# Self-attention P.V with two products instead of three, and a new order of work at the end and the start of each batch

## The chip, the cores and the metric

The kernel runs on one core of one Trainium2 chip. The metric is the device time of one execution in microseconds (us). TensorE (PE) multiplies, VectorE (DVE) and ScalarE (ACT) read its results out of the eight PSUM banks, GpSimd (POOL) works on SBUF alone, and SyncE (SP) issues the DMAs. Each engine runs its own list of instructions in order; semaphores tie the lists together.

## The reference, cut to what matters

The layer takes x (8 batches of 128 tokens, 512 features) and a context of the same size and computes

```
x = x + self_attention(layernorm(x))      # 32 query heads of 16, 8 key/value heads, rotary angles, causal
x = x + cross_attention(layernorm(x), ctx) # 32 query heads of 128, 4 key/value heads
x = x + ffn(layernorm(x))                  # two branches, one scaled by a routing weight, layer norm with gamma, beta
```

All data are float32. In the self-attention of one batch (the code splits its 32 heads into 8 groups j of 4 query heads that share one key/value head):

```
scores[h] = q[h] @ k[h // 4].T / 4, masked above the diagonal
attn[h]   = softmax(scores[h])
ctx[h]    = attn[h] @ v[h // 4]            # the product P.V
out       = concat(ctx) @ Wo.T
```

For the cross-attention, "latents" are the normalised rows of x after the self-attention; keys and values are made from the context rows followed by the latents, so every batch's latents must be turned (transposed) and multiplied by the key and value weights.

## The kernel before, in words

**Number format.** Every float32 operand a of a product is split into two fp32r parts: the high part h, which ScalarE's copy rounds, and the low part l = a - h, which VectorE makes from the same PSUM bank. `split3` (L235 to L239) then issues three matmuls: high by high (L237), high by low, low by high. So each PSUM result that is used again costs one ScalarE copy (L1285) and one VectorE subtraction (L1597).

**Phases.** The kernel has a start (weights and context are turned), the self-attention in 8 batches (`batch(b, last)` in each engine's list, about 98 to 290 us), the cross-attention in 128 steps, and the ffn. The change touches only the start and the 8 batches.

**One batch on TensorE (L890 to L988).** Eight steps j. Step j turns the normalised probabilities of group j (`turn(j)`, L903, four 128x128 transposes into bank 5 or 6), then does other work of the batch, then `values(j-1)`: the product P.V of the group before, into bank 7. The values lie block-diagonally in `Vbdh` and `Vbdl`, so that the 128 output rows are filled by the eight groups one after the other, and each group costs a `split3` of 512 columns (for j = 7, two of 256 columns, each as soon as its half of the low part `PTal` is there). The other work:

- step 0: `unit(U_B0 + 2 * b)` (12 matmuls: cross-attention values of the batch's context rows, XTh and XVh in the rows), then `turn_xn(b + 1)` (L789: the next batch's normalised x into bank 0), then `scores(b, 2)`;
- steps 2 to 4: `q_product`, `scores(b, 3)` and `kv_product` (next batch's queries, keys, values);
- steps 6 and 7: `turn_q` and `turn_k` (L810, L817) of the next batch, into banks 1 and 4;
- after step 7: `values(7)`, `scores(b + 1, 0)`, the output product (12 matmuls with `SOh`, into bank 6), `scores(b + 1, 1)`, the tail unit `unit(U_B0 + 2 * b + 1)` (12 matmuls, XTh and XKh in the rows), and `turn_latents(b)` (L829: the rows xn2 into bank 0).

`scores(b, m)` (L856 to L874) starts two banks with the mask (L864, two matmuls) and adds three products of 64 rows each for both halves (L868, L871, L874, two matmuls each); it uses the banks 2, 3 and 4 in turn.

**The followers.** ScalarE's list for a batch (L1352 to L1379): for each j the high part `PTah` of the turned probabilities, then the exponentials `probs(b, j + 3)` (four activations, each with an accumulator read, L1342); in step 0 also the high parts of the unit and of `turn_xn`; after step 7 the high part of the keys, of the attention output (OTh) and of the values, `probs(b + 1, 0..2)`, the high part of the tail unit and of the latents. VectorE's list (L1729 to L1796): for each j the row maxima (L1721), the low part `PTal`, the reciprocals of the sums (L1727); the rotary products; after step 7 the low parts of the keys, their block-diagonal copies `Kbdl` (L1696, four per batch), the low part of the output OTl, `maxima(b + 1, 0)` and `(b + 1, 1)`, the low part of the values. Then VectorE waits for the output product, adds it to x (L1785), takes the statistics (L1629 to L1633), and only then `reciprocals_a(b + 1, 1)` and `maxima(b + 1, 2)` (L1789), the normalised rows xn2 (L1791), two more `Kbdl`, and the low parts of the tail unit and of the latents. GpSimd multiplies the probabilities by the reciprocals (L635), makes the high block-diagonal keys `Kbdh` (L620) and the inverse standard deviations (L600, L651).

**The last batch** has no next batch: its steps 1, 2 and 4 to 7 hold units of the earlier latents instead (`LAST_STEPS`, L451), and after the tail unit come `first_queries(0)` and `turn_latents(7)`.

Of the kernel before, what the change touches and what calls it, by code (L numbers as in the profile page):

```python
# [29 lines left out]
ALU = mybir.AluOpType  # L30
# [34 lines left out]
def decoder_layer(nc, x, ctx, s_wq, s_wk, s_wv, s_wo, x_wq, x_wk, x_wv, x_wo, gate_w, up_w, down_w,  # L65
                  fc1_w, fc2_w, expert_w, gamma, beta, rope, out):
    with ExitStack() as stack:
# [74 lines left out]
        VBW = P + SD  # L142
        Vbdh = sb("Vbdh", "F", 0, [SKV * VBW], F32R)
        Vbdl = sb("Vbdl", "F", 4.5, [SKV * VBW], F32R)
        OTh, OTl = PTah[:, 0, :], PTal[:, 0, :]
# [108 lines left out]
        v_ptl_half, v_ol_half = sem("v_ptl_half"), sem("v_ol_half")  # L254
# [211 lines left out]
        def _(sp):  # L466
# [52 lines left out]
            sp.wait_ge(pe_pv, NB)  # L519
# [66 lines left out]
        def _(gp):  # L586
# [51 lines left out]
            def batch(b, last):  # L638
                for j in range(2, SKV):
                    normalise(b, j)  # L640
                    if j == 3 and b + 2 < NB:
                        inv_std1(b + 2)
# [128 lines left out]
        def _(pe):  # L771
# [84 lines left out]
            def scores(b, m):  # L856
# [6 lines left out]
                for bk, _ in halves:  # L863
# [8 lines left out]
                pe.wait_ge(v_kbd, KC * b + m + 1)  # L872
# [17 lines left out]
            def batch(b, last):  # L890
# [16 lines left out]
                def values(j):  # L907

                    if j == SKV - 1:
                        for n, split in enumerate((v_ptl_half, v_ptl)):  # L910
                            pe.wait_ge(split, SKV * b + SKV if n else b + 1)
                            cols = slice(n * KEYS, (n + 1) * KEYS)
                            op = split3(pe, bank[7][:, cols], Vbdh[:, j * P:(j + 1) * P], Vbdl[:, j * P:(j + 1) * P],
                                        PTah[:, j % 2, cols], PTal[:, j % 2, cols], False, n == 1)
# [3 lines left out]
                    if j == 0:  # L918
# [3 lines left out]
                    op = split3(pe, bank[7][:], Vbdh[:, j * P:(j + 1) * P], Vbdl[:, j * P:(j + 1) * P],  # L922
                                PTah[:, j % 2, :], PTal[:, j % 2, :], j == 0, False)

                for j in range(SKV):
                    turn(j)
                    if j == 0:
# [41 lines left out]
                else:  # L969
                    unit(U_L0 + 6)  # L970

                for g in range(SG):
                    if g % 2 == 0:
                        pe.wait_ge(v_ol if g else v_ol_half, b + 1)
# [1096 lines left out]
```

## Time and profile before

| | us |
|---|---|
| median of 3 runs (lowest, highest) | 1007.47 (1006.96, 1007.87) |
| time of the profiled execution | 1007.5 |
| its span, first to last instruction | 1005.8 |
| mean granted TensorE clock | 0.999 |

The span is what the trace shows; 1.7 us of the profiled execution's own time lie around it. The profile page gives each engine's busy time. A busy TensorE is not TensorE at its peak, since matmuls overlap and their ends are modelled: the distance from one start to the next says what a matmul costs. "mean ns of one" is therefore longer than the cost of a matmul in a row of many.

### The profile page before, as it was taken

What the parts mean: (1) busy time and instruction counts of PE and PEld (TensorE: products, weight loads), DVE (VectorE), ACT (ScalarE), POOL (GpSimd) and SP (SyncE); (2) the same over time, 40 slices, a digit from 0 to 9 for tenths busy, and PEclk for the clock granted to TensorE, in tenths of its full rate; (3) what the DMA queues carried; (4) which work ended last, traced back from release to release, by engine and by line L of the source; (5) the groups of instructions that cost most, each with busy time, mean ns of one, the idle gap of its engine ahead of it and who ended that gap; (6) DMA issues with size and microseconds to landing.
All of it is one profiled execution on the core that took longest, in us unless ns stands there. A gap on an engine that the chain in (4) does not pass through costs nothing.

```text
span 1005.8 us, 16102 instructions
## 1 busy us (share of the span) xinstructions
PE 995.6 (99%) x5552; PEld 836.7 (83%) x5552; DVE 641.4 (64%) x1224; ACT 559.5 (56%) x1695; POOL 519.8 (52%) x529
## 2 busy tenths in 40 slices
PE   8999999999999999999999999999999999999997
PEld 7777777777788888888888888888888888899996
DVE  6888888888433786555655655555555566655654
ACT  5766667666534665555656556555655667422221
POOL 3645444444231786665755756576666568512220
PEclk9999999999999999999999999999999999999999
DMA  9410111104454313233213313322332245100000
GB/s 343 119 29 15 43 42 44 42 22 124 135 157 119 95 57 102 74 95 105 86 61 105 105 64 106 92 76 94 95 105 75 83 139 168 62 22 21 21 22 21
DMA packets 74857, 85.15 MB, mean 85 GB/s; under 512 B 4512, under 2 KB 54688, under 8 KB 74784
## 3 DMA queue, kind: packets, MB, share of 16 engines
q1 hardware_dynamic: 74784, 84.21, 26.2%
q8 instruction: 42, 0.69, 0.3%
q14 instruction: 31, 0.25, 0.1%
HBM read 65.32 MB, written 18.87 MB: 84 GB/s over the span
## 4 chain that ended last, share of the span: by engine, by line
PE 92%; DVE 3%; ACT 2%; DMA 1%; issue 1%; POOL 1%; SPq 1%; DVEq 0%; POOLq 0%; ACTq 0%
PE bank L237 23%; PE bank L239 22%; PE bank L238 22%; PE bank L1143 11%; PE bank L1187 5%; PE bank L903 3%; PE bank L864 1%; PE bank L868 1%; DMA rawO<-in_L_attn_Wo_dram 1%; PE bank L871 1%; PE bank L874 1%; ACT Pb L1424 0%; DVE Kbdl L1696 0%; PE bank L817 0%; PE bank L810 0%
## 5 line engine op out<-in xcount | busy, mean ns | idle before, releaser
L673 POOL TENSOR_TENSOR Pb<-Pb,b_rec 128x512 f32<-128x512 f32 x128 | 135.5, 1059 | 200.6 <-DVE b_rec L1848 200.5
L1424 ACT ACTIVATE Pb<-bank,b_nb 128x256 f32<-128x256 f32 x256 | 119.1, 477 | 14.3 <-DVE b_nb L1843 14.2
L1843 DVE TENSOR_REDUCE b_nb<-bank 128x2 f32<-128x512 f32 x128 | 88.1, 688 | 59.2 <-PE bank L239 58.4
L635 POOL TENSOR_TENSOR Pa<-Pa,a_rec 128x512 f32<-128x512 f32 x64 | 68.2, 1066 | 102.1 <-DVE a_rec L1727 101.5
L1342 ACT ACTIVATE Pa<-bank,a_nb 128x128 f32<-128x128 f32 x256 | 90.8, 370 | 45.5 <-DVE a_nb L1721 44.8
L1285 ACT ACTIVATE PTh<-bank 128x512 fp32r<-128x512 f32 x128 | 76.3, 596 | 67.1 <-PE bank L1187 67.1
L237 PE MATMUL bank<-WOh,Oh 128*128 128x512 f32 x256 | 111.3, 435 | 0.0
L1597 DVE TENSOR_TENSOR PTl<-bank,PTh 128x512 fp32r<-128x512 f32 x128 | 87.7, 686 | 22.3 <-ACT PTh L1285 22.2
L239 PE MATMUL bank<-WOh,Ol 128*128 128x512 f32 x256 | 101.0, 395 | 0.0
L238 PE MATMUL bank<-WOl,Oh 128*128 128x512 f32 x256 | 100.4, 392 | 0.0
L1285 ACT ACTIVATE Oh<-bank 128x512 fp32r<-128x512 f32 x64 | 38.3, 599 | 91.4 <-PE bank L239 91.4
L1597 DVE TENSOR_TENSOR Ol<-bank,Oh 128x512 fp32r<-128x512 f32 x64 | 44.2, 690 | 63.1 <-ACT Oh L1285 63.1
L1187 PE MATMUL bank<-ident,Pb 128*128 128x128 f32 x512 | 76.8, 272 | 0.0
L239 PE MATMUL bank<-KV,Ql 128*128 128x256 f32 x256 | 72.4, 283 | 0.0
L238 PE MATMUL bank<-KV,Qh 128*128 128x256 f32 x256 | 72.3, 282 | 0.0
L237 PE MATMUL bank<-KV,Qh 128*128 128x256 f32 x256 | 71.8, 281 | 0.0
L1187 PEld LDWEIGHTS bank<-ident,Pb 128*128 128x128 f32 x512 | 61.4, 140 | 8.8 <-POOL Pb L673 0.2
L1285 ACT ACTIVATE PTah<-bank 128x512 fp32r<-128x512 f32 x72 | 43.4, 603 | 32.2 <-PE bank L903 24.1
L679 POOL TENSOR_TENSOR rstd<-var_eps,half 128x1 f32<-128x1 f32 x16 | 12.3, 767 | 92.4 <-DVE var_eps L1633 92.4
L1597 DVE TENSOR_TENSOR PTal<-bank,PTah 128x512 fp32r<-128x512 f32 (+1 forms) x88 | 50.3, 587 | 11.3 <-ACT PTah L1285 10.6
L239 PEld LDWEIGHTS bank<-WOh,Ol 128*128 128x128 f32 x256 | 48.0, 188 | 11.3
L1424 ACT ACTIVATION_READ_ACCUMULATOR Pb<-bank,b_nb 128x1 f32 x256 | 53.6, 210 | 0.0
(279 smaller groups left out, 3008.6 us busy)
## 6 DMA issues: line engine op xcount, KB each, us to landing
KV<-kv_scratch SPq DMA_DIRECT2D x64, 512.0 KB, 3.4
kv_scratch<-KVst SPq DMA_DIRECT2D x64, 256.0 KB, 3.1
raw<-in_L_xattn_Wo_dram SPq DMA_DIRECT2D x32, 256.0 KB, 3.9
raw<-in_L_xattn_Wq_dram SPq DMA_DIRECT2D x24, 256.0 KB, 3.2
cx<-in_ctx_dram SPq DMA_DIRECT2D x8, 256.0 KB, 8.9
raw_first<-in_L_xattn_Wq_dram SPq DMA_DIRECT2D x8, 256.0 KB, 4.6
raw<-in_L_ffn_up_w_dram SPq DMA_DIRECT2D x8, 256.0 KB, 3.9
raw<-in_L_ffn_down_w_dram SPq DMA_DIRECT2D x8, 256.0 KB, 3.5
```

What stands on the lines that cost most here:

```text
L237: pe.matmul(dst, lh, rh, start=start, stop=False)
L238: pe.matmul(dst, lh, rl, start=False, stop=False)
L239: return pe.matmul(dst, ll, rh, start=False, stop=stop)
L635: gp.tensor_tensor(pj, pj, a_rec[:, SG * j:SG * j + SG].unsqueeze(2).to_broadcast([P, SG, P]), ALU.mult).then_inc(g_norm, 1)
L673: gp.tensor_tensor(pk, pk, b_rec[:, k % 4, :].unsqueeze(2).to_broadcast([P, 2, KEYS]), ALU.mult).then_inc(b_g_norm, 1)
L1143: op = pe.matmul(bank[6][:], lhs[:, p, kc, :], rhs[:, kc, :], start=p in (0, 4, 5) and kc == 0 and n_op == 0, stop=kc == 1 and n_op == 2, ...
L1187: op = pe.transpose(bank[3 + k % 2][:, c * KEYS + h * P:c * KEYS + (h + 1) * P], Pb[:, k % 4, h, c * P:(c + 1) * P], ident[:])
L1285: return act.activation(dst, src, ACT.Copy)
L1342: op = act.activation(Pa[:, j % PS, c * P:(c + 1) * P], bank[2 + j % 3][:, c * P:(c + 1) * P], ACT.Exp, bias=a_nb[:, h:h + 1], scale=1.0, ...
L1424: op = act.activation(Pb[:, k % 4, h, :], bank[k % 3][:, h * KEYS:(h + 1) * KEYS], ACT.Exp, bias=b_nb[:, k % 4, h:h + 1], scale=1.0, accum ...
L1597: return dve.tensor_tensor(dst, src, f32(hi_part), ALU.subtract)
L1843: dve.tensor_reduce(b_nb[:, k % 4, :], bank[k % 3][:].rearrange("p (h k) -> p h k", h=2), AX.X, ALU.max, negate=True).then_inc(b_v_nb, 1)
```

## The change

**Two products instead of three.** One tile `Vst` holds, for each group j, the high values in the 16 columns of row block j and the low values 64 columns further (for j < 4) or 64 columns nearer (for j >= 4). One product of `Vst` with `PTah` and one with `PTal` then give the high part's result in one half of the bank's partitions and the low part's result in the other half. Groups 0 to 3 go to bank 7 and groups 4 to 7 to bank 4. The low half must be moved by 64 partitions and added: ScalarE copies it out (`OLa`, `OLb`), and `add_low(n)` multiplies it with a shifted identity `swap_r` of 64 rows and adds it into the other half of the same bank. The high and low parts of the output are then made for the two halves separately.

**Order.** The tail unit goes ahead of the output product. `turn_latents(b)` leaves the end of batch b for step 0 of batch b + 1; it stands behind the unit and waits until the low part of the turned x (`v_xnl`) has left bank 0. `turn_xn` goes ahead of the unit. Keys are turned into bank 3. SP's load of the gate and expert weights waits for the last output product.

**GpSimd** makes the fourth low diagonal block (m = 3), behind `normalise(b, 2)`.

```diff
         # turn_k, scores
+                if b:
+                    pe.wait_ge(a_exp, SKV * b)
-                    op = pe.transpose(bank[4][:, m * P:(m + 1) * P], kr[:, m * P:(m + 1) * P], ident[:])
+                    op = pe.transpose(bank[3][:, m * P:(m + 1) * P], kr[:, m * P:(m + 1) * P], ident[:])
...
+                    if m == 0 and n:
+                        pe.wait_ge(v_qkl, 2 * b + 2)
+                    if m == 1 and n == 0 and b:
+                        pe.wait_ge(v_ol, 2 * b)
...
         # values, TensorE
+                    bk = bank[7] if j < 4 else bank[4]
...
-                    op = split3(pe, bank[7][:], Vbdh[:, j * P:(j + 1) * P], Vbdl[:, j * P:(j + 1) * P],
-                                PTah[:, j % 2, :], PTal[:, j % 2, :], j == 0, False)
+                    if j == 4:
+                        pe.wait_ge(a_exp, SKV * b + 6)
+                    pe.matmul(bk[:], Vst[:, j, :], PTah[:, j % 2, :], start=j % 4 == 0, stop=False)
+                    op = pe.matmul(bk[:], Vst[:, j, :], PTal[:, j % 2, :], start=False, stop=j == 3)
+                    if j == 3:
+                        op.then_inc(pe_pv, 1)
+
+                def add_low(n):
+                    pe.wait_ge(a_ol, 2 * b + n + 1)
+                    bk, rows, low = ((bank[7], UPPER, OLa), (bank[4], LOWER, OLb))[n]
+                    pe.matmul(bk[:], swap_r[rows, :], low, start=False, stop=True,
+                              skip_group_check=True).then_inc(pe_sw, 1)
...
         # step 0, TensorE
-                        unit(U_B0 + 2 * b)
+                        pe.wait_ge(v_vl, b + 1)
                         if not last:
-                            if b:
-                                pe.wait_ge(v_htl, b)
-                            else:
+                            if b == 0:
                                 pe.wait_ge(v_ctl, 6)
                             turn_xn(b + 1)
+                        unit(U_B0 + 2 * b)
+                        if b:
+                            if not last:
+                                pe.wait_ge(v_xnl, b + 2)
+                            turn_latents(b - 1)
                         scores(b, 2)
...
+                    if j == 6:
+                        add_low(0)
...
         # after step 7, TensorE
+                add_low(1)
+                tail = U_E0 - 1 if last else U_B0 + 2 * b + 1
+                pe.wait_ge(v_ol, 2 * b + 1)
+                if b:
+                    pe.wait_ge(v_htl, b)
+                unit(tail)
+                pe.wait_ge(v_ol, 2 * b + 2)
                 for g in range(SG):
...
                 if not last:
                     scores(b + 1, 1)
-                unit(U_E0 - 1 if last else U_B0 + 2 * b + 1)
-                if not last:
-                    pe.wait_ge(v_vl, b + 2)
-                else:
+                if last:
                     first_queries(0)
                     pe.wait_ge(v_ul, U_L0 + 7)
-                turn_latents(b)
+                    turn_latents(b)
...
         # ScalarE, batch
+                    if j == 0 and not last:
+                        xn_hi(b + 1)
+                    if j == 5:
+                        act.wait_ge(pe_pv, 2 * b + 1)
+                        hi(OLa, bank[7][UPPER, :]).then_inc(a_ol, 1)
+                    if j == 7:
+                        if not last:
+                            k_hi(b + 1)
+                        act.wait_ge(pe_sw, 2 * b + 1)
+                        hi(OTh[LOWER, :], bank[7][LOWER, :]).then_inc(a_o, 1)
                     if j + 3 < SKV:
                         probs(b, j + 3)
                     if j == 0:
                         unit_hi(U_B0 + 2 * b)
-                        if not last:
-                            xn_hi(b + 1)
+                        if b:
+                            latents_hi(b - 1)
...
-                act.wait_ge(pe_pv, b + 1)
-                hi(OTh, bank[7][:]).then_inc(a_o, 1)
+                act.wait_ge(pe_pv, 2 * b + 2)
+                hi(OLb, bank[4][LOWER, :]).then_inc(a_ol, 1)
                 if not last:
                     values_hi(b + 1)
+                act.wait_ge(pe_sw, 2 * b + 2)
+                hi(OTh[UPPER, :], bank[4][UPPER, :]).then_inc(a_o, 1)
...
         # VectorE, batch
+                    if j == 0 and not last:
+                        ln1_lo(b + 1)
                     if j < 4:
                         reciprocals_a(b, j + 2)
                     if j == 0:
                         unit_lo(U_B0 + 2 * b)
+                        if b:
+                            latents_lo(b - 1)
...
-                    diagonal_keys(b + 1, (2, 3))
+                    diagonal_keys(b + 1, (2,))
                 unit_lo(U_E0 - 1 if last else U_B0 + 2 * b + 1)
-                latents_lo(b)
+                if last:
+                    latents_lo(b)
```

VectorE's wait for the output product, the addition, the statistics and `maxima(b + 1, 2)` behind them stay in their order.

## Rows read from the trace of the kernel before

**Rows 1.** The page's first part: each engine's busy time, share and instructions.
```profile
PE 995.6 (99%) x5552; PEld 836.7 (83%) x5552; DVE 641.4 (64%) x1224; ACT 559.5 (56%) x1695; POOL 519.8 (52%) x529
```

**Rows 2.** Busy time by stretch, one batch; then clock, DMA share and GB/s.
```profile
157.90:187.80 29.90, 29.89 (x170) 23.05 (x169) 25.81 (x56) 20.18 (x80) 14.08 (x14) 1.00 0.13 36
```

**Rows 3.** TensorE's groups by shape, whole span: count | busy us, mean ns.
```profile
L239 PE MATMUL bank<-PTah,Vbdl 128*128 128x512 f32 x56 | 22.0, 393 | 0.0
L239 PE MATMUL bank<-PTah,Vbdl 128*128 128x256 f32 x16 | 4.5, 282 | 0.0
```

**Rows 4.** Timeline, TensorE, end of a batch and start of the next: start, duration.
```profile
180.14 0.40 PE L874 MATMUL bank<-Kbdl,QTh 64*128 64x512 f32 x2
180.47 0.50 PE L237 MATMUL bank<-SOh,PTah 128*128 128x512 f32 x1
...
183.10 0.39 PE L239 MATMUL bank<-SOh,PTal 128*128 128x512 f32 x1
183.32 0.61 PE L864 MATMUL bank<-mask_r,ident_r 128*128 128x512 f32 x2
...
184.76 0.50 PE L237 MATMUL bank<-XTh,XKh 128*128 128x512 f32 x1
...
187.62 0.60 PE L829 MATMUL bank<-ident,xn 128*128 128x128 f32 x4
...
188.05 0.60 PE L903 MATMUL bank<-ident,Pa 128*128 128x128 f32 x4
188.41 0.47 PE L237 MATMUL bank<-XVh,XTh 128*128 128x512 f32 x1
...
191.24 0.60 PE L789 MATMUL bank<-ident,xn 128*128 128x128 f32 x4
191.59 0.71 PE L864 MATMUL bank<-mask_r,ident_r 128*128 128x512 f32 x2
```

**Rows 5.** Timeline of VectorE over the same stretch.
```profile
183.52 0.69 DVE L1785 TENSOR_TENSOR x_res<-x_res,bank 128x512 f32<-128x512 f32 x1 [0.36 <-PE bank L239]
...
185.49 0.66 DVE L1721 TENSOR_REDUCE a_nb<-bank 128x4 f32<-128x512 f32 x1
...
187.33 1.28 DVE L1696 TENSOR_TENSOR Kbdl<-KTl,bd_mask 128x512 fp32r<-128x512 f32 x2
188.53 0.68 DVE L1597 TENSOR_TENSOR KVst<-bank,KVst 128x512 fp32r<-128x512 f32 x1
189.13 0.68 DVE L1597 TENSOR_TENSOR XTl<-bank,XTh 128x512 fp32r<-128x512 f32 x1
```

**Rows 6.** Timeline of ScalarE over the same stretch.
```profile
186.18 0.37 ACT L1342 ACTIVATE Pa<-bank,a_nb 128x128 f32<-128x128 f32 x1 [1.76 <-DVE a_nb L1721]
...
187.48 0.22 ACT L1342 ACTIVATION_READ_ACCUMULATOR Pa<-bank,a_nb 128x1 f32 x1
187.81 0.60 ACT L1285 ACTIVATE KVst<-bank 128x512 fp32r<-128x512 f32 x1
```

**Rows 7.** Timeline of all engines, step 7 of the same batch.
```profile
176.45 0.60 PE L903 MATMUL bank<-ident,Pa 128*128 128x128 f32 x4
...
177.08 0.60 ACT L1285 ACTIVATE PTah<-bank 128x512 fp32r<-128x512 f32 x1 [0.59 <-PE bank L903]
...
177.58 0.59 ACT L1285 ACTIVATE KTh<-bank 128x512 fp32r<-128x512 f32 x1
177.71 0.76 DVE L1597 TENSOR_TENSOR PTal<-bank,PTah 128x256 fp32r<-128x256 f32 x2 [0.32 <-ACT PTah L1285]
...
178.19 0.39 PE L237 MATMUL bank<-PTah,Vbdh 128*128 128x256 f32 x1
178.24 1.04 POOL L620 TENSOR_TENSOR Kbdh<-KTh,bd_mask 128x512 fp32r<-128x512 f32 x1 [2.98 <-ACT KTh L1285]
```

**Rows 8.** Timeline of the last batch's end: last output matmul, normalised rows.
```profile
284.35 0.39 PE L239 MATMUL bank<-SOh,PTal 128*128 128x512 f32 x1
287.40 1.50 DVE L1791 TENSOR_SCALAR xn<-x_res,mv,rstd 128x512 f32<-128x512 f32 x1 [0.67 <-POOL rstd L651]
```

More of the change, by code:

```diff
@@ L141, in decoder_layer @@
         mask_f = sb("mask_f", "ST", 7.5, [P])
[L142 to L145, printed above, removed]
+        Vst = sb("Vst", "F", 0, [SKV, P], F32R)
+        OTh = sb("OTh", "F", 4, [D], F32R)
+        OTl = sb("OTl", "F", 6, [D], F32R)
+        swap_r = sb("swap_r", "ST", 6, [P], F32R)
+        LOWER, UPPER = slice(0, 64), slice(64, P)
+        OLa, OLb = OTl[UPPER, :], PTah[LOWER, 0, :]
         rope_q1 = sb("rope_q1", "WQ", 12, [KC, P])
@@ L871, in scores @@
                     pe.matmul(bk[:], QTl[rows, m, :], Kbdh[rows, m, :], start=False, stop=False)
-                pe.wait_ge(v_kbd, KC * b + m + 1)
+                if m < KC - 1:
+                    pe.wait_ge(v_kbd, (KC - 1) * b + m + 1)
+                else:
+                    pe.wait_ge(g_kbl, b + 1)
                 for bk, rows in halves:
@@ L912, in values @@
                             cols = slice(n * KEYS, (n + 1) * KEYS)
-                            op = split3(pe, bank[7][:, cols], Vbdh[:, j * P:(j + 1) * P], Vbdl[:, j * P:(j + 1) * P],
-                                        PTah[:, j % 2, cols], PTal[:, j % 2, cols], False, n == 1)
+                            pe.matmul(bk[:, cols], Vst[:, j, :], PTah[:, j % 2, cols], start=False, stop=False)
+                            op = pe.matmul(bk[:, cols], Vst[:, j, :], PTal[:, j % 2, cols], start=False, stop=n == 1)
                         op.then_inc(pe_pv, 1)
@@ L1313, in k_hi @@
                 act.wait_ge(pe_qk, 2 * b + 2)
-                hi(KTh[:], bank[4][:].rearrange("p (k n) -> p k n", k=KC)).then_inc(a_qk, 1)
+                hi(KTh[:], bank[3][:].rearrange("p (k n) -> p k n", k=KC)).then_inc(a_qk, 1)
             def context_hi(b):
@@ L1681, in values_lo @@
                 dve.wait_ge(a_v, b + 1)
-                vv = [t[:].rearrange("p (j c) -> p j c", c=VBW)[:, :, 0:SD] for t in (Vbdl, Vbdh)]
-                lo(vv[0], bank[0][:, P:2 * P].rearrange("p (j d) -> p j d", j=SKV), vv[1]).then_inc(v_vl, 1)
+                cells = Vst[:].rearrange("p a (b d) -> p (a b) d", d=SD)
+                for n in range(2):
+                    js = slice(4 * n, 4 * n + 4)
+                    first = 4 * n * (SKV + 1)
+                    at_lo = first + (-4 if n else 4)
+                    op = lo(cells[:, at_lo:at_lo + 3 * (SKV + 1) + 1:SKV + 1, :],
+                            bank[0][:, P:2 * P].rearrange("p (j d) -> p j d", j=SKV)[:, js, :],
+                            cells[:, first:first + 3 * (SKV + 1) + 1:SKV + 1, :])
+                op.then_inc(v_vl, 1)
             def q_lo(b):
@@ L1690, in k_lo @@
                 dve.wait_ge(a_qk, 2 * b + 2)
-                lo(KTl[:], bank[4][:].rearrange("p (k n) -> p k n", k=KC), KTh[:]).then_inc(v_qkl, 1)
+                lo(KTl[:], bank[3][:].rearrange("p (k n) -> p k n", k=KC), KTh[:]).then_inc(v_qkl, 1)
             def diagonal_keys(b, ms):
@@ L1770, in batch @@
                     diagonal_keys(b + 1, (0,))
-                dve.wait_ge(a_o, b + 1)
-                for n, done in enumerate((v_ol_half, v_ol)):
-                    cols = slice(n * KEYS, (n + 1) * KEYS)
-                    lo(OTl[:, cols], bank[7][:, cols], OTh[:, cols]).then_inc(done, 1)
+                dve.wait_ge(a_o, 2 * b + 1)
+                lo(OTl[LOWER, :], bank[7][LOWER, :], OTh[LOWER, :]).then_inc(v_ol, 1)
+                dve.wait_ge(a_o, 2 * b + 2)
+                lo(OTl[UPPER, :], bank[4][UPPER, :], OTh[UPPER, :]).then_inc(v_ol, 1)
                 if not last:
```

35 lines of the change are left out of this document (19 added, 16 removed).

## The prediction

> **What bounds the kernel now.** I read four views, in this order. The page's first part says that TensorE is busy for 995.6 of 1005.8 us [rows 1]. The stretches by batch say the same of the part that the change touches: in one batch TensorE is busy for 29.89 of 29.90 us, VectorE for 25.81, ScalarE for 20.18 and GpSimd for 14.08, at a granted clock of 1.00, the 2.4 GHz level [rows 2]. So TensorE sets the pace of the batches, hardly ever waits, and each matmul taken out is worth its own spacing, as long as nothing else becomes late. The third view, the timeline of TensorE, gives these spacings and the order [rows 4]; the batch repeats every 29.83 us. The fourth, the timelines of the followers, says how long the chain is that leads from a matmul through VectorE and ScalarE back to TensorE, and how much matmul work covers it now [rows 5 to 7].
>
> **What the two-pass product takes out.** The third product of `split3` for P.V goes: 56 matmuls of 512 columns and 16 of 256 [rows 3], 7 and 2 per batch. A 512-column matmul in a row of many costs 2.83 us / 12 = 0.236 us with the first one's weight change, 2.63 / 11 = 0.239 us in the output product, where the last one's own time isn't in [rows 4]; from one to the next inside a row it is 0.23 us (2.83 less about 0.31 for the first, over 11). The two of 256 columns make one more. That is 8 x 0.23 = 1.84 us per batch.
>
> **What it adds to TensorE.** Two `add_low` per batch, a single product of 64 rows and 512 columns; no row shows one alone. Two such together end 0.33 us before the next kind of matmul starts (180.14 to 180.47) [rows 4]. Half of that, 0.17, is the bound from below; two such steps with a change of kind on either side, 0.66, bound it from above. I take 0.33, the row of the nearest shape: 0.66 us per batch. Net -1.84 + 0.66 = -1.18 us per batch, if nothing waits.
>
> **Waits in the last steps of a batch.** Step 7 is a chain already: `turn(7)` starts at 176.45, its copy PTah at 177.08, the half low part at 177.71, `values(7)` at 178.19 [rows 7], 1.74 us. In between stand `turn_k` and `values(6)`, which get shorter by 0.23, so TensorE only waits longer. The same holds behind it: the copy KTh starts at 177.58, 0.50 after PTah on the same engine, the first Kbdh at 178.24 and takes 1.04, and `scores(b + 1, 0)` can't go on before. ScalarE's new copy OLa stands between the copies of steps 5 and 6 and takes another 0.50 there. Its second mask matmul waits for the low keys, VectorE's next piece, which ends about when the first Kbdh does. I put what the chain takes back at 0.3 to 0.6 us per batch, from one to two and a half of the shortened products, and take 0.5. Below: 0, if the copies run ahead; above: 0.92, all four products of steps 4 to 7. The last batch has units of 12 matmuls in these steps and loses none.
>
> **What the new order does.** Here lies the main term. Take the last output matmul (start 183.10) as zero. Today VectorE adds the product at +0.42; statistics and a reciprocal come next; the row maxima of `scores(b + 1, 1)` start at +2.39 [rows 5]; ScalarE's exponentials start at +3.08 and their last accumulator read at +4.38, so that its next copy can start at about +4.47 [rows 6]. TensorE doesn't notice, since it has scores (1.44), tail unit (2.86), `turn_latents` (0.43), `turn(0)` (0.36), unit (2.83) and `turn_xn` (0.35) ahead of it [rows 4], 8.49 us up to `scores(b, 2)`.
>
> After the change the tail unit (2.86 us) is behind the zero no longer, while VectorE's and ScalarE's lists still have the whole chain in it, and TensorE waits at its end: `turn_latents(b - 1)` overwrites bank 0 and needs `v_xnl`. That chain goes, on ScalarE: exponentials until +4.47, high part of the tail unit +4.47, PTah of step 0 at +4.97, high part of x at +5.46 (0.50 from copy to copy [rows 7]). On VectorE: Kbdl at +4.23, one now instead of two; the low part of the tail unit needs its high part (0.60 long [rows 6]) and starts at +5.10; then, 0.60 apart as at 188.53 and 189.13 [rows 5], the maxima at +5.70, PTal of step 0 at +6.30, and the low part of x at +6.90, which ends at +7.58. TensorE goes on at +7.65. It has come there at 1.66 + 0.43 + 0.35 + 2.83 = +5.27 (scores with the last matmul, `turn(0)`, `turn_xn`, unit) [rows 4]. It waits 7.65 - 5.27 = 2.38 us.
>
> Every step of this chain is a row of before, in the order that the lists keep, so I give it little room: 2.0 us if two of the VectorE pieces close up, 2.9 if the normalised xn2, already stretched by GpSimd's work beside it, stretches further. In batch 0 there are no latents to turn and no wait; batches 1 to 6 have it, 6 x 2.38 = 14.3 us. In the last batch `turn_latents(6)` has no such wait, but the next unit (`LAST_STEPS[1]`) needs the latents' low part, `v_htl`. Behind the low part of step 0's PTal (+6.30) come a reciprocal and the low part of the unit, whose high part waits for exponentials that start with the maxima's end (+6.4) and take 1.39: +7.80 and +8.43. Then the low part of the latents at +9.03 to +9.71. TensorE comes to it at 1.66 + 0.43 + 2.83 + 0.43 + 1.45 + 0.41 = +7.2 (with `turn_latents`, scores and `turn(1)`) and waits 2.5 us.
>
> At the end of that batch the rows xn2 are started 3.05 us after the last output matmul and take 1.50 [rows 8]: +4.55. Before, tail unit and `first_queries` (5.5 us) lay over this; now only `first_queries`, 0.23 + 2.72 = 2.95. Another 1.6 us of waiting.
>
> **The rest.** The turns of `turn_latents` are moved, not added: 0. One Kbdl leaves VectorE (0.60) and comes to GpSimd (1.04), behind `normalise(b, 2)`, where GpSimd now stands idle until VectorE's next reciprocal; `scores(b, 3)` needs it 5 us later: 0, and 1.04 per batch if `normalise(b, 3)` were late. VectorE's wait chain above doesn't gain by it, since the tail unit's high part (+5.07) is later than Kbdl's end (+4.87). The Trainium skill ("GPSIMD Engine Reference", 1. Specifications) says that GpSimd shares its SBUF interfaces with VectorE and gets in the way of VectorE's instructions that have two SBUF inputs. By this rule the moved piece would cost nothing, as VectorE's neighbours there read PSUM, and the last batch's 1.50 us for xn2 would be shorter if GpSimd's first_wq_lo came later, up to about 1 us; the sum does not use it. ScalarE's two further copies (0.60 each; 0.27 as the bound from below) and VectorE's split of the values stand beside units of 2.8 us: 0. SP's gate and expert loads wait for the last output product; stores behind them are needed more than 10 us later: 0. The start loses one memset and gains two small copies: 0, bound by 0.3 either way.
>
> **Sum.** Batches 0 to 6: 7 x (-1.18 + 0.5) = -4.8. Batch 7: -1.2. New waits: +14.3 + 2.5 + 1.6 = +18.4. In all +12.4 us, on the profiled execution's own 1007.5 us (span 1005.8), which is the median of the runs, 1007.47. The cross-attention behind it starts later by as much and gives nothing back, since TensorE runs without a wait there too. That is 1019.9; I take 1019.5, as step 0's wait also gives VectorE time to catch up. Own range 1015 to 1024: the wait between 2.0 and 2.9 (-2.3, +3.1), `add_low` between 0.17 and 0.66 (-2.6, +5.3), the last steps between 0 and 0.92 (-3.5, +2.9), not all at one end.
>
> **Rivals.**
>
> *The cover is enough (faster).* If the low part of x is there when TensorE arrives, the kernel keeps -4.8 - 1.2 = -6.0, or up to -9.4 without the waits in the last steps: 998 to 1002, 1001 for one number. For it: TensorE is full and followers have 4 us idle per batch [rows 2], and the low part of x now stands early in step 0. Against: it stands behind the statistics of the output product in both lists. The point from which it decides is a wait of about (6.0 / 7 =) 0.9 us per batch; below it the change wins. My chain is 2.38, so it would have to be shorter by 1.5 us. Chance 0.14.
>
> *Half of it.* The exponentials or the low parts run ahead by 1 us (the maxima before the statistics, say, or a copy order that I misread): 12.4 - 7 = +5 or less, 1007 to 1014, 1011 for one number. Chance 0.10.
>
> *The clock falls.* In the batches the granted clock is 1.00 with TensorE never at rest [rows 2]; the new waits put it at rest 8 times for some 2 us. If it dropped to the lower level (1.2 GHz) behind them, 512 columns would cost twice 0.23, and each 3 us of matmul work at that level another 3 us; one such stretch per wait adds 8 x 3 = 24 us: 1040. No row of before shows a fall next to a wait, so the chance is small, 0.04. The Trainium skill ("TensorE: Matmul & The Clock Gate", Part 1) says that the clock is halved after the array has been idle for a while, which speaks against any change that adds waits; by it the time would be 1040, or as in the sum if these waits are too short for it.
>
> *More waits.* The added copies also make `turn(j)` late in steps 2 to 6 (1 us per batch): 1024 to 1029. Chance 0.07.
>
> My forecast has the remaining 0.65. The smallest difference that a measurement of this kernel tells from none is about 0.2%, 2 us. Faster by more holds the first rival and a part of the second, 0.14 + 0.03 = 0.17; within 0.2% a part of the second, 0.05; slower the rest, 0.78. The range that leaves out two in ten is 1007 to 1025: it takes in the second rival and nearly all of my own, and leaves out the first, the clock's and the upper half of the last.
>
> **What would show it.** On TensorE's timeline the mean batch is 31.5 us (29.83 - 1.18 + 0.5 + 2.38) for batches 1 to 6 and about 29.2 for batch 0. A gap of 2.4 us stands ahead of `turn_latents` in step 0, its releaser the low part xnTl on VectorE, and the last output matmul lies 7.65 us ahead of the gap's end. VectorE's maxima still start 2.4 us after the last output matmul. The P.V groups show 64 x 2 matmuls, and `add_low` 0.33 each. The last batch shows a wait for XTl of about 2.5 us and one for xn of about 1.6. Step 7's `values` still start 1.7 us after `turn(7)`. I am wrong if step 0 shows no gap, or a gap under 0.9 us, if the granted clock is below 1.00 in the batches, or if the cross-attention's length changes by more than 1 us.

## The result, and the profile after

| | before | after |
|---|---|---|
| median, us (lowest, highest) | 1007.67 (1006.96, 1008.30) | 1029.40 (1028.51, 1032.34) |
| profiled execution's own time, span | 1007.5, 1005.8 | 1028.82, 1027.1 |
| mean granted TensorE clock | 0.999 | 0.994 |

The changed kernel is slower: ratio 1.0215, 95% interval 1.0202 to 1.0228. The sign and the place of the waits are as forecast, the size isn't: +12 us were forecast, with 1025 as the upper end, and it is +21.7. (The section on the kernel before says that the batches begin at about 98 us. They begin earlier: `turn(0)` of batch 0 starts at 37.7.)

First TensorE in the page's first part, then the list of what TensorE waited for (total us, times, longest). Before, its longest wait inside the batches was 0.2 us.

```profile
PE 996.3 (97%) x5496; PEld 830.3 (81%) x5496; DVE 639.1 (62%) x1225; ACT 570.0 (55%) x1719; POOL 527.4 (51%) x537
```

```profile
PE bank L845 <- DVE xnTl L1656: 12.8, 6, 2.1
PE bank L242 <- DVE XTl L1656: 2.3, 1, 2.3
...
PE bank L802 <- DVE xn L1702: 2.0, 1, 2.0
PE bank L939 <- DVE PTal L1656: 1.7, 7, 0.2
PE bank L845 <- DVE xn L1861: 1.6, 1, 1.6
```

There are 56 matmuls fewer (5496 against 5552 [rows 1]), and yet the busy time is no shorter: part of the matmuls ran at a lower clock (4.3 us, below), and short rests that the modelled ends of matmuls cover count as busy. The forecast waits are there: six ahead of `turn_latents` (L845), one for XTl, one for xn in the last batch. The one for PTal is step 7's chain, as forecast: TensorE waits about 0.2 us longer ahead of `values(7)` than before, and `values(7)` starts 1.75 us behind `turn(7)` as it did. The wait of 2.0 us at L802, ahead of `turn_xn` in batch 0, was not forecast.

The timeline of TensorE at the start of batch 2, answering to [rows 4], and of VectorE and ScalarE, answering to [rows 5, 6]:

```profile
101.10 0.39 PE L244 MATMUL bank<-SOh,OTl 128*128 128x512 f32 x1
...
103.26 0.60 PE L802 MATMUL bank<-ident,xn 128*128 128x128 f32 x4
103.61 0.47 PE L242 MATMUL bank<-XVh,XTh 128*128 128x512 f32 x1
...
106.24 0.39 PE L244 MATMUL bank<-XVh,XTl 128*128 128x512 f32 x1
108.74 0.66 PE L845 MATMUL bank<-ident,xn 128*128 128x128 f32 x4 [2.12 <-DVE xnTl L1656]
```

```profile
101.52 0.69 DVE L1855 TENSOR_TENSOR x_res<-x_res,bank 128x512 f32<-128x512 f32 x1 [1.89 <-PE bank L244]
...
103.48 0.66 DVE L1789 TENSOR_REDUCE a_nb<-bank 128x4 f32<-128x512 f32 x1
...
106.20 0.69 DVE L1656 TENSOR_TENSOR KVst<-bank,KVst 128x512 fp32r<-128x512 f32 x1 [0.21 <-ACT KVst L1332]
...
108.00 0.68 DVE L1656 TENSOR_TENSOR xnTl<-bank,xnTh 128x512 fp32r<-128x512 f32 x1
```

```profile
104.17 0.37 ACT L1389 ACTIVATE Pa<-bank,a_nb 128x128 f32<-128x128 f32 x1 [3.36 <-DVE a_nb L1789]
...
105.56 0.61 ACT L1332 ACTIVATE KVst<-bank 128x512 fp32r<-128x512 f32 x1
106.04 0.61 ACT L1332 ACTIVATE PTah<-bank 128x512 fp32r<-128x512 f32 x1
106.52 0.62 ACT L1332 ACTIVATE xnTh<-bank 128x512 fp32r<-128x512 f32 x1
```

With the last output matmul (101.10) as zero, the maxima start at +2.38, the exponentials at +3.07, the copies at +4.46, +4.94 and +5.42, VectorE's pieces at +5.10 and +6.90, and TensorE goes on at +7.64. The forecast had +2.39, +3.08, +4.47, +4.97, +5.46, +5.10, +6.90 and +7.65. TensorE's last matmul ahead of it starts at +5.14; it stands still for 2.12 us.

What was not in the sum is the clock. By stretches of 2 us (busy times, then the granted clock before the DMA share and GB/s), these are two of the three places where it fell from 2.4 to 1.2 GHz; the third is at 42.3 us:

```profile
140.00:142.00 2.00, 1.54 (x8) 1.17 (x10) 1.22 (x4) 1.75 (x7) 1.44 (x2) 0.85 0.68 202
142.00:144.00 2.00, 2.00 (x11) 1.26 (x9) 1.25 (x2) 0.00 (x0) 0.60 (x1) 0.50 0.54 157
144.00:146.00 2.00, 2.00 (x11) 1.58 (x11) 1.03 (x3) 1.75 (x8) 0.27 (x1) 0.79 0.35 105
206.00:208.00 2.00, 2.00 (x9) 0.86 (x8) 1.29 (x2) 0.62 (x2) 1.48 (x2) 0.57 0.23 68
208.00:210.00 2.00, 2.00 (x11) 1.73 (x10) 0.92 (x2) 0.86 (x4) 0.00 (x0) 0.58 0.78 229
```

Each follows a wait: TensorE had been still for 2.14 us up to 140.46, for 2.13 up to 205.33, for 1.96 up to 41.03 (the third fall, in batch 0). Not every wait is followed by one: two of the six ahead of `turn_latents` are. From one `turn_k` to the next a batch takes 31.70 us, and 33.14 and 33.11 where the clock fell, so one fall costs 1.43 us there.

**Where the 21.3 us of span went**, by TensorE's timelines. Up to `turn_k` in batch 0 the changed kernel is 2.71 us later (60.26 against 57.55): the start 0.77, the wait for xn 1.96, one fall 1.4 (the twelve products of the unit take 4.40 us instead of 3.01), `add_low(0)` 0.4, less 1.4 for six P.V products fewer and 0.4 for short rests that the kernel before had there. Then come six batches of 31.70 instead of 29.83 us, 11.2, and two falls, 2.9. The rest, 4.5, lies behind the last `turn_k`: the waits of 2.3 and 1.6 us in the last batch, a wait of 0.3 for a transfer in the cross-attention, and 0.3 that I can't place.

### The profile page after: what moved, and what is told of

Read it like the earlier page. It is cut to its first block, busy times and chain, and to the rows that moved or that the text cites. A ratio compares the mean times of both kernels' runs of the same rounds, so it can differ in the third digit from the quotient of the medians.

```text
span 1027.1 us, 16046 instructions
## 1 busy us (share of the span) xinstructions
PE 996.3 (97%) x5496; PEld 830.3 (81%) x5496; DVE 639.1 (62%) x1225; ACT 570.0 (55%) x1719; POOL 527.4 (51%) x537
## 4 chain that ended last, share of the span: by engine, by line
PE 86%; DVE 6%; ACT 3%; DMA 2%; issue 1%; POOL 1%; SPq 1%; DVEq 0%; POOLq 0%; ACTq 0%
PE bank L242 20%; PE bank L244 19%; PE bank L243 19%; PE bank L1190 11%; PE bank L1234 5%; PE bank L928 3%; PE bank L951 1%; PE bank L952 1%; ACT Pa L1389 1%; DMA rawO<-in_L_attn_Wo_dram 1%; PE bank L886 1%; PE bank L890 1%; DVE a_nb L1789 1%; DVE KVst L1656 1%; DVE stats L1689 1%
## 5 line engine op out<-in xcount | busy, mean ns | idle before, releaser
L1483 ACT ACTIVATE Pb<-bank,b_nb 128x256 f32<-128x256 f32 x256 | 118.9, 476 | 14.3 <-DVE b_nb L1914 14.2
L1332 ACT ACTIVATE PTah<-bank 128x512 fp32r<-128x512 f32 (+1 forms) x72 | 43.4, 603 | 25.7 <-PE bank L928 22.0
L1389 ACT ACTIVATION_READ_ACCUMULATOR Pa<-bank,a_nb 128x1 f32 x256 | 54.2, 212 | 0.0
```

Of the source, the lines that this page charges most:

```text
L1332: return act.activation(dst, src, ACT.Copy)
L1389: op = act.activation(Pa[:, j % PS, c * P:(c + 1) * P], bank[2 + j % 3][:, c * P:(c + 1) * P], ACT.Exp, bias=a_nb[:, h:h + 1], scale=1.0, ...
L1483: op = act.activation(Pb[:, k % 4, h, :], bank[k % 3][:, h * KEYS:(h + 1) * KEYS], ACT.Exp, bias=b_nb[:, k % 4, h:h + 1], scale=1.0, accum ...
```

## The experiments

All numbers are medians in us. The ratio is against the kernel before in the same run, and "falls" counts the stretches at the lower clock in the profiled execution (before: none; changed kernel: 3).

| kernel | time | ratio, 95% interval | batch | falls |
|---|---|---|---|---|
| a_tail_back | 1020.39 | 1.0129 (1.0112, 1.0145) | 30.95 | 1 |
| b_filler | 1025.58 | 1.0182 (1.0165, 1.0199) | 31.73 | 1 |
| c_xn0 | 1029.63 | 1.0214 (1.0197, 1.0231) | 31.73 | 5 |
| d_lat_later | 1021.56 | 1.0144 (1.0128, 1.0161) | 31.07 | 1 |
| e_order_alone | 1043.61 | 1.0359 (1.0343, 1.0375) | 32.63 | 7 |
| n_order_filler | 1032.90 | 1.0240 (1.0224, 1.0256) | 32.64 | 1 |
| g2_maxima_first | 1043.05 | 1.0352 (1.0337, 1.0368) | 32.8 | 6 |
| h_dve_diag | 1034.97 | 1.0265 (1.0249, 1.0281) | 32.04 | 6 |
| j_step7 | 1029.91 | one run | 31.73 | 4 |
| g1_half_tail | 1011.91 | 1.0038 (1.0025, 1.0052) | 30.30 | 0 |
| k_low_in_step7 | 1008.65 | 1.0004 (0.9995, 1.0013) | 29.85 | 0 |
| l_latents_step1 | 1004.58 | 0.9962 (0.9948, 0.9975) | 29.02 | 0 |

"batch" is the distance of two `turn_k` with no fall between them. For g2_maxima_first there is a fall in every such distance; 32.8 is 34.25 less 1.43.

**The order alone, on the kernel before.** Three products as before; tail unit ahead of the output product, `turn_latents(b - 1)` in step 0.

```diff
# before, after scores(b + 1, 0)
+                pe.wait_ge(v_ol, b + 1)
+                unit(tail)
                 # output product, scores(b + 1, 1)
-                unit(U_E0 - 1 if last else U_B0 + 2 * b + 1)
-                turn_latents(b)
# step 0
+                            turn_xn(b + 1)
                         unit(U_B0 + 2 * b)
-                            turn_xn(b + 1)
+                                pe.wait_ge(v_xnl, b + 2)
+                            turn_latents(b - 1)
```

> The kernel before with the new order alone: three products for P.V as before, but the tail unit ahead of the output product, turn_xn ahead of the unit, and turn_latents(b - 1) in step 0 behind the wait for the low part of x. Theory 1 (the order costs, whatever the products are): six waits of about 2.2 us ahead of turn_latents, 2.4 for XTl in the last batch, 1.6 and 2.0 for xn at the end and in batch 0, together 19 us, plus 3 to 10 us of stretches at the lower clock: 1029 to 1037. Theory 2 (it is the two-pass product with its copies): under 1012.

1043.6, above the forecast of theory 1 and far from theory 2. The waits are where they were expected, but add up to 22.0 us and not to 19: 2.45 us ahead of `turn_latents`, as in the changed kernel with both Kbdl on VectorE (h_dve_diag below), 2.7 for XTl, 3.0 and 1.6 for xn. The clock falls seven times. So this order costs 36 us without the two-pass product, and the rest of the change gives part of that back: the order carries the loss. What the two products and their copies give back is seen against h_dve_diag, which has the same two Kbdl: 32.04 us per batch against 32.63.

**The clock.** In the changed kernel (b_filler), and then in the kernel just described (n_order_filler), 8 matmuls that compute nothing were put into the waits of batches 0 to 6: ident_r by ident_r, into a bank that is overwritten next. The waits of the last batch stayed empty.

```diff
                             if not last:
+                                pe.wait_ge(a_exp, SKV * b + 2)
+                                filler(8, 3)
                                 pe.wait_ge(v_xnl, b + 2)
                             turn_latents(b - 1)
# and in batch 0
                             if b == 0:
+                                pe.wait_ge(a_exp, 2)
+                                filler(8, 3)
                                 pe.wait_ge(v_ctl, 6)
                             turn_xn(b + 1)
```

> The changed kernel with 8 matmuls of 512 columns that compute nothing (1.84 us at 2.4 GHz), put into the waits ahead of turn_latents (batches 1 to 6) and ahead of turn_xn in batch 0, where TensorE stood still for 1.96 to 2.13 us. Their results are overwritten. Theory 1: the granted clock fell to the lower level three times behind these waits (at 42.3, 141.7 and 206.9 us) because TensorE rested; with the fillers it stays at 1.00 in all batches and the three stretches, about 1.4 us each, come back: 1029.4 - 4.3 = 1025, and the spread between runs gets smaller. Theory 2: the clock fell for another reason (power, or chance): still falls, 1029.

> The kernel before with the new order alone (1043.6 us, seven stretches at the lower clock), with 8 matmuls that compute nothing in each of the waits of batches 0 to 6. Theory 1 (each stretch follows a rest of TensorE and costs 1.45 us): the stretches in batches 0 to 6 go, one may be left in the last batch, whose wait isn't filled: 1043.6 - 6 x 1.45 = 1034.9, or 1033.4 with none left. Theory 2 (the lower clock has another cause): 1043.

1025.6 and 1032.9. In both, no fall is left in batches 0 to 6, and the one that is left comes with the empty wait of the last batch. An undisturbed batch keeps its length (31.70 and 31.73; 32.63 and 32.64), so the fillers cost nothing there and what comes back is the clock. The stretches around that last fall in b_filler, behind a wait of 2.4 us for XTl:

```profile
PE bank L242 <- DVE XTl L1664: 2.4, 1, 2.4
```

```profile
266.00:268.00 2.00, 0.83 (x3) 0.68 (x4) 2.00 (x4) 1.02 (x3) 0.56 (x1) 0.92 0.27 73
268.00:270.00 2.00, 2.00 (x7) 1.52 (x6) 0.40 (x2) 1.25 (x8) 1.04 (x1) 0.50 0.63 190
```

**Batch 0.** `turn_xn` of batch 0 alone behind the unit.

```diff
-                        if not last:
-                            if b == 0:
-                                pe.wait_ge(v_ctl, 6)
+                        if b and not last:
                             turn_xn(b + 1)
                         unit(U_B0 + 2 * b)
+                        if b == 0:
+                            pe.wait_ge(v_ctl, 6)
+                            turn_xn(b + 1)
```

> The changed kernel, with turn_xn of batch 0 alone put back behind the unit. Theory 1: the wait of 1.96 us for xn and the stretch at the lower clock behind it (1.4 us) go: 1029.4 - 3.4 = 1026.0. Theory 2 (batch 0 is late for another reason, and the wait only moves): under 1 us of gain.

The wait is gone, the time isn't: 1029.6. Theory 1's 1026.0 is missed, and theory 2 has the number. The list of waits has no L802, but the clock falls five times instead of three, none of them in batch 0. In batch 0 itself, from `turn(0)` to `turn_k`, the kernel takes 19.18 us against 21.78. Of these 2.60, 1.6 are the fall (the unit takes 2.82 us against 4.40), so only 1.0 of the wait's 2.0 comes back: `turn(2)` and `turn(3)` now come 0.4 and 0.8 us later behind the turn ahead of them, with rests for GpSimd's Pa. So the wait for xn covered another chain in part. All five falls lie behind waits that the changed kernel has too, and why the clock falls behind more of them here, no run shows. The number of falls differs between executions of one kernel too, as the changed kernel's own runs suggest: 1028.51, 1029.98 and 1032.34 go with mean clocks of 0.994, 0.992 and 0.990.

**The tail unit behind the output product again.**

```diff
-                pe.wait_ge(v_ol, 2 * b + 1)
-                unit(tail)
                 pe.wait_ge(v_ol, 2 * b + 2)
                 # output product, scores(b + 1, 1)
+                unit(tail)
```

> The changed kernel with one part of its order undone: the tail unit stands behind the output product and scores(b + 1, 1) again. Theory 1 (the order took the cover of VectorE's and ScalarE's chain): the six waits of 2.1 us ahead of turn_latents, the 2.3 us for XTl in the last batch and the 1.6 us for xn go. But the output product now follows add_low(1) at once and must wait for the upper low part OTl: that ended 1.75 us after add_low(1) began, the product came 0.32 us after it, so 1.45 us of waiting in each of 8 batches, 11.6. Time 1029.4 - 13.6 - 3.9 + 11.6 = 1023.5, and about 3 to 4 less, 1020, if the clock stays up because the waits are shorter. Theory 2 (the two-pass product and its four copies are what costs, the order is neutral): 1029.

1020.4, as forecast by theory 1, and with the waits that it named:

```profile
PE bank L242 <- DVE OTl L1654: 11.3, 8, 1.4
PE bank L1038 <- DVE ident_r L1657: 2.1, 1, 2.1
PE bank L802 <- DVE xn L1700: 2.0, 1, 2.0
```

The wait ahead of `turn_latents` is gone, and the output product waits 1.4 us for the upper OTl in each of 8 batches. So the tail unit has two places, each of which covers one chain and bares the other.

**Another cover: `turn_latents` behind `scores(b, 2)`.**

```diff
-                            turn_latents(b - 1)
                         scores(b, 2)
+                            turn_latents(b - 1)
```

Its wait for `v_xnl` goes with it.

> The changed kernel, with scores(b, 2) ahead of turn_latents(b - 1) and its wait for the low part of x, so that 1.54 us of matmuls cover this wait. Theory 1: the wait shrinks from 2.12 to about 0.6 us in batches 1 to 6 (-9.2) and the clock no longer falls in them (-2.8): 1029.4 - 12.0 = 1017.4. Theory 2: the chain of the followers slips by as much as TensorE gains, because the row maxima and copies behind it are what sets the pace: 1027 to 1029.

1021.6, a gain of 7.8 instead of 12. The waits fell to 0.8 us, but a new one came, 0.5 us in six batches, for GpSimd's probabilities ahead of `turn(3)`:

```profile
PE bank L845 <- DVE xnTl L1656: 4.8, 6, 0.8
PE bank L928 <- POOL Pa L642: 2.8, 6, 0.5
```

**The maxima ahead of the statistics on VectorE.**

```diff
-                norm_stats(x_res[:, b, :], v_st2)
                 if not last:
                     reciprocals_a(b + 1, 1)
                     maxima(b + 1, 2)
+                norm_stats(x_res[:, b, :], v_st2)
```

> The changed kernel with VectorE's maxima(b + 1, 2) (and the reciprocal ahead of it) in front of the statistics of the output instead of behind them: the chain to the low part of x starts earlier. Theory 1: the maxima can start when scores(b + 1, 1) has its first half, 1.8 us after the last output matmul instead of 2.4, so the wait ahead of turn_latents falls from 2.1 to 1.5 us in six batches and by as much in the last: -4.2 us; 1025, with 2 us to either side for the number of stretches at the lower clock. Theory 2 (the low part of x is held by another part of the chain, xn2 and Kbdl on VectorE): no gain, 1029.

Worse than both theories: 1043.1, waits of 3.2 us. The exponentials do start earlier (2.50 us behind the last output matmul instead of 3.07), but now VectorE stands still for GpSimd's inverse deviation, and xn2 and Kbdl come late in front of the tail unit's low part. VectorE's timeline:

```profile
104.05 0.69 DVE L1689 BATCH_NORM_STATS2 stats<-x_res 128x6 f32<-128x512 f32 x1
...
105.90 1.25 DVE L1861 TENSOR_SCALAR xn<-x_res,mv,rstd 128x512 f32<-128x512 f32 x1 [0.66 <-POOL rstd L664]
...
107.67 0.68 DVE L1656 TENSOR_TENSOR KVst<-bank,KVst 128x512 fp32r<-128x512 f32 x1
```

Behind the last output matmul (101.50) the low part of the tail unit starts at +6.17 instead of +5.10, and that is the 1.07 us by which the wait grew. In the old order the maxima filled the time that VectorE now waits.

**The fourth low diagonal block back on VectorE.** GpSimd's `if j == 2:` part, which makes it, is taken out.

```diff
-                    pe.wait_ge(g_kbl, b + 1)
+                    pe.wait_ge(v_kbd, KC * b + m + 1)
-                    diagonal_keys(b + 1, (2,))
+                    diagonal_keys(b + 1, (2, 3))
```

> The changed kernel with the fourth low diagonal block back on VectorE, two in a row behind xn2. Theory 1: on VectorE the second Kbdl ends at +5.5 behind the last output matmul instead of +4.9, 0.4 us behind the point where the high part of the tail unit is ready (+5.1), so the wait ahead of turn_latents grows by 0.4: 6 x 0.4 = 2.4 us, 1031.8, with 3 us to either side for the number of stretches at the lower clock. Theory 2 (the move to GpSimd is neutral): the waits stay at 2.12 us.

The waits ahead of `turn_latents` are 2.45 us and the batch 32.04, 0.34 more; the wait for xn in batch 0 grew to 3.4, and there were six falls: 1035.0. So that part of the change helped, by 0.34 us in each of six batches and 1.4 in batch 0, before the clock.

**The chain in step 7.** Two matmuls that compute nothing (0.46 us) ahead of `values(6)`.

```diff
+                    if j == 7 and not last:
+                        pe.wait_ge(a_exp, SKV * b + 7)
+                        filler(2, 2)
                     values(j - 1)
```

> The changed kernel with two matmuls of 512 columns that compute nothing (0.46 us) ahead of values(6) in batches 0 to 6, where the products were shortened. Theory 1 (turn(7), its copies and GpSimd's first Kbdh are a chain, so what is saved there is lost again): an undisturbed batch grows from 31.70 to at most 31.9 us. Theory 2 (TensorE's own work counts there): to 32.16 us.

An undisturbed batch takes 31.73 to 31.76 us against 31.70, theory 1. From `turn_k` to the first product of `scores(b + 1, 0)` it is 2.67 us with the two (L917) and 2.66 without (123.66 to 126.32 in the changed kernel):

```profile
90.34 0.60 PE L833 MATMUL bank<-ident,kr 128*128 128x128 f32 x4
90.70 0.71 PE L917 MATMUL bank<-ident_r 128*128 128x512 f32 x2
...
93.01 0.50 PE L890 MATMUL bank<-Kbdh,QTh 64*128 64x512 f32 x2
```

In the kernel before, it was 2.69 with three products in each of the groups. What the two-pass product saved behind `turn_k` was worth nothing.

**A version that covers both chains.** Half of the tail unit on each side of the output product, `turn_latents` behind `scores(b, 2)`, batch 0's `turn_xn` behind its unit, the last batch's units from step 2 on:

```diff
-                unit(tail)
+                unit(tail, (0, 1))
                 # output product, scores(b + 1, 1)
+                unit(tail, (2, 3))
```

> The two-pass product with an order that covers both chains: half of the tail unit (6 matmuls, 1.4 us) between add_low(1) and the output product, the other half behind scores(b + 1, 1); turn_latents(b - 1) behind scores(b, 2); turn_xn of batch 0 behind the unit; in the last batch the units of the earlier latents begin in step 2 instead of 1. Theory 1: the waits go (1.4 us of matmuls ahead of the output product against 1.45 of wait, 1.4 + 1.5 ahead of turn_latents against 2.3), the clock stays up: 1007.6 less what the two-pass product is worth without them. The run with the tail unit put back gives that as 1020.4 - 1.7 (one stretch at the lower clock) - 2.0 (xn) - 11.3 (OTl) = 1005.4. So 1005, faster than both. Theory 2: turn(2) then waits for GpSimd's normalisation (0.5 us in six batches when turn_latents alone was moved), and the total is no better than before: 1008 to 1010.

1011.9, not 1005. No fall, no wait for xnTl or OTl, and still 0.47 us per batch more than before. The wait for GpSimd's Pa ahead of `turn(3)` is there, 0.5 us, and steps 5 to 7 are longer than they were: from `turn(5)` to the first product of `scores(b + 1, 0)` 6.14 us against 5.94. Next, `add_low(0)` from step 6 to step 7, ahead of `values(6)`:

```diff
-                    if j == 6:
+                    if j == 7:
                         add_low(0)
```

> The kernel with half of the tail unit on each side (its batch takes 30.30 us), and add_low(0) moved from step 6 to step 7, ahead of values(6), where two idle matmuls of 512 columns had cost only 0.04 us per batch. Theory 1 (steps 5 to 7 are a chain through ScalarE and VectorE, with room for TensorE only behind turn(7)): add_low(0) with its change of kind, 0.42 us, leaves the chain and costs nothing in its new place; 7 x 0.4 = 2.8 us, 1011.9 - 2.8 = 1009.1, batch 29.9 us. Theory 2 (TensorE's total work sets the pace there): no change, 1011.9.

1008.7 and a batch of 29.85, as theory 1 had it: in step 6 the added product stood in the chain, in step 7 it is hidden. Last, `turn_latents` behind `turn(1)`, and its two copies behind those of step 1:

```diff
-                        if b:
-                            latents_hi(b - 1)
...
+                    if j == 1 and b:
+                        latents_hi(b - 1)
```

> The kernel before this one in the list, and turn_latents behind turn(1), with ScalarE's and VectorE's copies of it behind the copies of step 1 instead of ahead of them. Theory 1: turn(1) and its chain (copy, low part, reciprocal, GpSimd) start 0.4 us earlier and nothing stands in front of them, so the wait of 0.46 us for GpSimd's probabilities ahead of turn(3) goes: 7 x 0.35 = 2.5 us, 1006.6, batch 29.55 us. Theory 2: exponentials of step 1 start 0.5 us later behind the moved copy and the wait shows in step 4: 1009.

1004.6, faster than both kernels (ratio to before 0.9962, interval 0.9948 to 0.9975). The gain of the last step is 4.1 us instead of 2.5: the batch is 29.02. The list of waits has the Pa wait 2 times with 0.4 us together, where g1 had 3.2 us in 8. Of the 0.83 us per batch, 0.78 lie between `turn(2)` and `turn(3)` (2.28 us instead of 3.06): that chain cost more than the 0.47 that the list gives, since it also stretched the products ahead of the wait. In the last batch a wait of 1.3 us for XTl came in return. No run has three products in this last order, so how much of its gain is the product's isn't shown. A batch shows TensorE without rest and at the full clock:

```profile
86.87:115.89 29.02, 29.02 (x162) 21.92 (x161) 25.46 (x56) 21.41 (x83) 15.09 (x15) 1.00 0.13 38
```

## Why the prediction was right about the waits and wrong in its size

Three steps of the prediction failed. The clock was left out of the sum, and three falls cost 4.3 us. Batch 0 was given no wait, and it has one of 1.96 us. The chain in the last steps was given 0.5 us per batch, and it took 0.7 to 0.8. The sign of being wrong that the prediction set itself, a granted clock below 1.00 in the batches, came. Without the falls the time would be about 1025, at the upper end of the range; with the fillers in the waits it was 1025.6.

- **Products taken out, `add_low` added.** The counts are right. `add_low(0)` costs 0.42 us and makes the turn ahead of it 0.08 longer (step 6), `add_low(1)` 0.24 net, since the change of kind was there before: 0.74 against the 0.66 taken, which was chosen between bounds far apart.
- **Waits in the last steps of a batch: mis-sized.** "I put what the chain takes back at 0.3 to 0.6 us per batch ... and take 0.5." Without its wait (2.27 us from the expected to the real start) a batch is 29.83 - (31.70 - 2.27) = 0.40 us shorter, not 0.68: the chain took 0.7, or 0.8 with the 0.08 that `add_low` costs more. ScalarE's copy OLa is part of it: the PTah behind it starts 0.83 us after its turn, those of the steps on either side 0.63. j_step7 and k_low_in_step7 show why: what stood in step 6 counted whole (0.45 us per batch), what stood behind `turn(7)` counted nothing.
- **What the new order does: right in batches 1 to 7.** 12.8 us of rest in six waits, 13.6 by starts, for 14.3; 2.3 for 2.5; 1.6 for 1.6. e_order_alone shows that it doesn't hang on the two-pass product.
- **"In batch 0 there are no latents to turn and no wait": wrong.** There is a wait of 1.96 us, for xn. The turn came 2.8 us earlier there, behind nothing but `turn(0)`, and the trace of before had the answer. VectorE's xn of batch 1 and TensorE's `turn_xn`, kernel before:

```profile
40.65 0.54 DVE L1642 TENSOR_SCALAR xn<-x_res,mv,rstd 128x512 f32<-128x512 f32 x1
```

```profile
41.33 0.63 PE L789 MATMUL bank<-ident,xn 128*128 128x128 f32 x4
```

  From the end of the one (41.19) to the start of the other there were 0.14 us. I had read one batch of the middle and taken it for all. c_xn0 adds that the wait was worth 1.0 us and not its whole length.
- **The clock: left out of the sum, the largest single miss.** It was put beside the forecast with a chance of 0.04, at 8 falls of 3 us each; the 3 us came from no row. It has three falls of about 1.43 us, 4.3 us, and belonged into the sum: it comes on top of the waits, not in their place. A fall costs 1.4 and not 3, since the lower clock lasts only for seven or eight products at 0.43 us instead of 0.23. The Trainium skill ("TensorE: Matmul & The Clock Gate", Part 1) says that idleness brings the lower clock. The traces agree in the direction (no fall without a wait of 1.4 us or more, none where the wait was filled); that waits of about 2 us came with a fall in some batches and not in others is what they add.
- **The rest.** The start is 0.77 us later (bound: 0.3). `turn(0)` of batch 0 starts at 38.48 instead of 37.71, and the transfer of the first value weights lands 4.7 us after its issue instead of 3.4. In the profiles of the other twelve kernels `turn(0)` starts between 36.6 and 39.1, so this is likely chance, but no run tested it.

Forecast terms corrected this way: 13.6 + 2.3 + 1.6 for the waits, 2.0 for batch 0, 4.3 for the clock, -2.8 for the shorter products in seven batches and 0.8 at the start make 21.8, against 21.3 of span. The agreement is closer than the terms: batch 0's 2.0 counts some 1 us too much by c_xn0, and the 1.2 less that the forecast gave the last batch isn't in the sum and isn't seen in its timeline.

The other rivals: the cover was not enough by 2.1 us and not by less than 0.9, VectorE's list did not run ahead, and the waits ahead of `turn(j)` in steps 2 to 6 did not come, though the time came out near that rival's 1029.

## What to carry to other kernels

Where an engine is busy for 99% of the time, independent work on it is at the same time the cover for a chain on the others: before a block of it is moved, write down the chain that it covered (here from the last output matmul to the low part of x, 7.6 us) and count what is left. Do that for the first and last iteration too, not for one of the middle alone. And a saving counts only outside the chains: with both covers in place, eight products shorter by a third gave nothing (29.85 us per batch against 29.83) until `turn_latents` and its two copies were taken out of one more chain, and then 0.8 us per batch.

## What the runs showed of the hardware

- TensorE's clock fell to its lower level behind waits of 1.4 to 3.4 us, but not behind each, and more often behind the longer ones. Over the batches of the kernels in the table and the changed one, 8 of 8 waits of 3.0 to 3.4 us came with a fall, 15 of 21 of 2.3 to 2.7, 11 of 23 of 1.9 to 2.2, none of nine of 1.56, one of eight of 1.41. None fell without such a wait, and none in the waits that were filled. Each fall made a batch 1.4 to 1.6 us longer. In the changed kernel's fall at 42.3 us, the distance between matmuls of 512 columns goes from 0.23 to 0.43 us; timeline of TensorE:

```profile
43.26 0.63 PE L242 MATMUL bank<-XVh,XTh 128*128 128x512 f32 x1
43.69 0.63 PE L243 MATMUL bank<-XVl,XTh 128*128 128x512 f32 x1
```

- Matmuls of 64 rows, two of them on different halves, took 0.23 us together (L893), no more than one of 128 rows. A single one between full-height ones (`add_low`, L960) took 0.42 us up to the next start in step 6, and 0.32 behind other products of 64 rows. Changed kernel:

```profile
122.23 0.49 PE L960 MATMUL bank<-OTl,swap_r 64*128 64x512 f32 x1
122.65 0.50 PE L951 MATMUL bank<-PTah,Vst 128*128 128x512 f32 x1
...
126.66 0.39 PE L893 MATMUL bank<-Kbdh,QTl 64*128 64x512 f32 x2
126.89 0.39 PE L899 MATMUL bank<-Kbdl,QTh 64*128 64x512 f32 x2
127.13 0.39 PE L960 MATMUL bank<-PTah,swap_r 64*128 64x512 f32 x1
127.45 0.50 PE L242 MATMUL bank<-XTh,XKh 128*128 128x512 f32 x1
```

- ScalarE's copy of 64 partitions by 512 elements took 0.59 us, about as long as one of 128 partitions (0.61, above); changed kernel:

```profile
121.44 0.59 ACT L1332 ACTIVATE OTl<-bank 64x512 fp32r<-64x512 f32 x1
```
